# New places for every step of a fused cross-attention and mixture-of-experts kernel, and a second buffer for the softmax quotients

## The reference

```
x = x + xattn(layernorm(x), ctx, ctx)      # 16 heads of 16 features, one shared k and v
   c = concat([ctx, ctx]); k, v = split(c @ w_kv); softmax(q k / 4) v @ w_concat
x = x + ffn(layernorm(x))
   a = layer_norm(x) * nw + nb
   expert = argmax(softmax(a @ wg))        # 8 experts, 256 places each, in order of the tokens
   moe = gate * (gelu(a[expert's tokens] @ inter_w[e] + inter_b[e]) @ output_w[e] + output_b[e])
   res = gelu(a @ res_inter_w + b1) @ res_output_w + b2          # residual MLP, all tokens
   out = res * coef0 + moe * coef1 + x     # coef = softmax(a @ res_coef)
```

## Time and profile before

| | |
|---|---|
| median of 3 runs | 447.14 us (445.47 to 448.82) |
| profiled execution | 447.72 us, of which the trace's span is 446.0 us |
| busy share of the span | PE 86%, PEld 66%, DVE 32%, ACT 38%, POOL 34% |
| TensorE clock granted, mean | 0.924 of full |
| DMA | 49.78 MB, mean 112 GB/s |

### The profile page before, as it was taken

The page is one execution under the profiler, slowest core; times in us unless marked ns, Lnnn a source line. Parts: engine busy times, 40 slices in busy tenths (PEclk is TensorE's granted clock), DMA queues, the critical chain, the costliest instruction groups (busy, mean ns, idle before and its releaser), DMA issues.

```text
span 446.0 us, 5656 instructions
## 1 busy us (share of the span) xinstructions
PE 381.6 (86%) x1978; PEld 292.7 (66%) x1978; DVE 142.2 (32%) x461; ACT 167.6 (38%) x325; POOL 153.2 (34%) x219
## 2 busy tenths in 40 slices
PE   4767777778998788988988988889999899999992
PEld 2435245555676476576576566678888788888881
DVE  3263424532354354363364263241101010101020
ACT  3213334345255435534536525552243223332310
POOL 4322313218156238247238035265002121212122
PEclk9757666986999999998999999999999999999998
DMA  7678650230022462381411410085122775581212
GB/s 203 189 193 233 228 134 2 76 79 24 23 72 77 125 234 71 94 272 51 114 35 61 104 37 12 21 294 165 47 68 64 196 235 166 128 251 12 25 18 29
DMA packets 51331, 49.78 MB, mean 112 GB/s; under 512 B 4764, under 2 KB 48488, under 8 KB 51304
## 3 DMA queue, kind: packets, MB, share of 16 engines
q1 hardware_dynamic: 48232, 45.21, 33.2%
q0 software_dynamic: 3072, 4.21, 5.2%
HBM read 33.65 MB, written 15.63 MB: 111 GB/s over the span
## 4 chain that ended last, share of the span: by engine, by line
PE 65%; DMA 10%; ACT 8%; DVE 7%; issue 5%; POOL 2%; SPq 2%; DVEq 0%; POOLq 0%; ACTq 0%
PE mbank L776 20%; PE ubank L612 18%; PE mbank L612 11%; DMA drow<-dispatched 8%; PE mbank L607 4%; PE pbank L697 4%; ACT p L847 3%; PE sbank L665 3%; PE sbank L687 3%; DVE smax L977 3%; PE pbank L706 2%; DVE core L1021 2%; ACT h L890 1%; DMA wq_raw<-in_L_xattn_w_q 1%; ACT oT L791 1%
## 5 line engine op out<-in xcount | busy, mean ns | idle before, releaser
L890 ACT ACTIVATE h<-ubank,vecT 128x256 f32<-128x256 f32 x128 | 53.7, 471 | 131.7 <-PE ubank L612 131.7
L776 PE MATMUL mbank<-w2r,h 128*128 128x256 f32 x256 | 64.1, 390 | 0.5 <-ACT h L890 0.5
L612 PE MATMUL ubank<-ao,w1r 128*128 128x256 f32 x256 | 62.7, 393 | 0.0
L776 PE MATMUL mbank<-w2e,h 128*128 128x256 f32 x256 | 60.8, 379 | 0.0
L580 POOL DMA_INDIRECT out_rows<-yrow,rowid x16 | 24.8, 1548 | 103.7 <-DVE yrow L1097 73.5
L612 PE MATMUL ubank<-ao,w1e 128*128 128x256 f32 x256 | 60.0, 379 | 0.0
L776 PEld LDWEIGHTS mbank<-w2r,h 128*128 128x128 f32 x256 | 48.4, 194 | 12.8 <-issue 5.3
L612 PEld LDWEIGHTS ubank<-ao,w1r 128*128 128x128 f32 x256 | 49.4, 197 | 6.6
L612 PEld LDWEIGHTS ubank<-ao,w1e 128*128 128x128 f32 x256 | 48.5, 190 | 6.6
L776 PEld LDWEIGHTS mbank<-w2e,h 128*128 128x128 f32 x256 | 48.2, 190 | 6.3
L977 DVE TENSOR_REDUCE smax<-sbank 128x4 f32<-128x512 f32 x64 | 41.9, 685 | 26.5 <-PE sbank L665 26.2
(11 more groups left out here) (123 smaller groups left out, 438.1 us busy)
## 6 DMA issues: line engine op xcount, KB each, us to landing
w1e<-in_L_ffn_inter_w SPq DMA_DIRECT2D x8, 1024.0 KB, 4.9
w2e<-in_L_ffn_output_w SPq DMA_DIRECT2D x8, 1024.0 KB, 8.4
qstack<-dram_q SPq DMA_DIRECT2D x16, 384.0 KB, 4.6
dram_q<-qpart SPq DMA_DIRECT2D x8, 384.0 KB, 2.5
dispatched<-zrow SPq DMA_DIRECT2D x4, 516.0 KB, 5.4
drow<-dispatched SPq DMA_DIRECT2D x8, 258.0 KB, 8.3
xs<-in_x SPq DMA_DIRECT2D x8, 256.0 KB, 4.6
ctxs<-in_ctx SPq DMA_DIRECT2D x8, 256.0 KB, 4.7
```

The costliest lines, as they stand in the source:

```text
L612: last = nc.tensor.matmul(dst, w[kc], v[kc], start=(kc == 0), stop=(kc == len(w) - 1))
L776: last = nc.tensor.matmul(b[:, 0:D], h[:, n % 2, f, t * P:(t + 1) * P], w2[:, f, :], start=(f == 0), stop=(f == FC - 1))
L890: nc.scalar.activation(h[:, n % 2, f, :], place["up", n, c][:, j, :], ACT.Gelu_apprx_tanh, bias=vecT[:, col:col + 1]).then_inc(sem("gelu_d ...
```

## The change

All tables of places, the shifts per engine and the places of the weight loads get new numbers; no step is added or taken away, and no instruction of TensorE, ACT or POOL changes. `o_rec` becomes a double buffer, and VectorE waits, before the reciprocal of half n, for the product of half n - 2. The diff, with the tables for tiles 0 and 1 and four of the five shift tables left out:

```diff
-    PERIOD = 32.0
-    OWN = [0.0, 15.16, 39.23, 67.63]
+    PERIOD = 32.21
+    OWN = [0.0, 14.33, 41.69, 73.4]
...
     AT = {
-        "load": [-76.7], "ln1": [-54.8], "xn": [-52.25], "ctxT": [-41.9], "xT": [-40.87], "kv": [-40.43],
-        "q": [-38.6], "qrest": [-38.13], "qmid": [-37.44], "qlast": [-34.08], "vt": [-34.97],
-        "A": [-16.17, -16.03, -13.98, -13.7, -12.14, -10.48, -10.21, -9.82], "M": [-14.15, -7.57],
-        "B": [-0.63, 1.24, 3.97, 4.13, 7.09, 8.2, 10.73, 12.79],
-        "PV": [5.63, 14.29], "part": [7.43, 16.09], "o": [7.83, 16.49], "oT": [17.79],
-        "proj": [18.79], "ln2": [21.72], "core": [23.76], "gate": [30.12], "loc": [39.86], "gw": [16.86],
-        "bias": [23.76], "up": [17.62, 19.37, 22.16, 25.97],
-        "down": [-0.9, 1.07, 1.42, 4.34, 7.37, 8.31, 11.9, 14.56], "kspill": [-35.58],
-        "qspill": [-39.35, -37.87, -37.05], "gather": [-31.09, -28.45],
+        "load": [-79.74], "ln1": [-63.27], "xn": [-50.13], "ctxT": [-48.04], "xT": [-45.19], "kv": [-42.33],
+        "q": [-40.39], "qrest": [-40.09], "qmid": [-39.1], "qlast": [-39.74], "vt": [-37.99],
+        "A": [-18.06, -16.74, -15.42, -14.72, -13.92, -13.31, -11.95, -10.83], "M": [-34.32, -10.5],
+        "B": [-0.44, 0.05, 2.98, 3.65, 6.41, 7.29, 8.23, 11.35], "PV": [7.09, 14.78], "part": [12.73, 16.11],
+        "o": [11.31, 15.15], "oT": [17.9], "proj": [19.56], "ln2": [18.73], "core": [23.68], "gate": [28.22],
+        "loc": [36.57], "gw": [12.03], "bias": [-27.15], "up": [17.29, 20.49, 22.55, 25.66],
+        "down": [-0.66, 0.71, 0.83, 4.43, 5.56, 9.79, 11.69, 15.58], "kspill": [-42.25],
+        "qspill": [-41.17, -41.04, -31.06], "gather": [-34.12, -28.45],
     }
...
     LAG_SP = {
-        "load": [0.0], "kspill": [0.18], "qspill": [0.0], "gather": [0.0], "M": [0.0], "wload": [0.0],
-        "ein": [0.0], "down": [0.25], "zero": [0.0], "late": [-0.64],
+        "load": [-3.06], "kspill": [-1.11], "qspill": [0.29], "gather": [3.78], "M": [-0.96], "wload": [1.51],
+        "ein": [1.22], "down": [0.86], "zero": [0.25], "late": [0.96], "small": [7.41], "end": [-1.82],
     }
     LOADS = {
-        "late": [-70.79], "vec": [-39.4], "zero": [-46.04, -45.13, -6.03, -0.66],
-        "weights": [0.5, 14.17, 15.87, 27.03, 27.11],
+        "late": [-103.98], "vec": [-54.72], "zero": [-67.38, -31.9, -9.19, 21.09],
+        "weights": [24.83, 27.63, 29.55, 73.96, 85.37],
     }
...
-        "period": 17.22, "up": [-2.35, 2.53, 4.67, 9.02],
-        "down": [17.16, 18.79, 20.45, 21.34, 23.58, 25.85, 26.32, 28.49], "ein": [9.47], "first": [-3.51],
+        "period": 23.05, "up": [-7.01, -6.86, -4.49, 0.18],
+        "down": [7.0, 10.93, 19.81, 20.46, 25.14, 25.66, 26.43, 28.03], "ein": [21.21], "first": [-4.28],
...
-        o_rec = sb("o_rec", [P, HB, HB], f32, att)
+        o_rec = sb("o_rec", [P, 2, HB, HB], f32, att)
...
-                V.reciprocal(o_rec[:, :, :], b[:, :, :, DH]).then_inc(sem("o_root"), 1)
+                if n >= 2:
+                    dve.wait_ge(sem("o_ready"), n - 1)
+                V.reciprocal(o_rec[:, n % 2, :, :], b[:, :, :, DH]).then_inc(sem("o_root"), 1)
```

More of the change, by code:

```diff
@@ L61, in xattn_moe_ffn_kernel @@
     AT0 = {
-        "load": [-77.76], "ln1": [-59.31], "xn": [-52.55], "ctxT": [-55.73], "xT": [-54.86], "kv": [-39.85],
-        "q": [-39.27], "qrest": [-41.07], "qmid": [-36.79], "qlast": [-29.31], "vt": [-38.49],
[3 rows of a table removed]
[L67 to L70, removed]
+        "load": [-44.59], "ln1": [-98.81], "xn": [-67.28], "ctxT": [-88.29], "xT": [-57.74], "kv": [-36.77],
@@ L71, in xattn_moe_ffn_kernel @@
+        "q": [-36.83], "qrest": [-47.74], "qmid": [-31.9], "qlast": [-34.13], "vt": [-30.08],
[4 rows of a table added]
+        "down": [-3.0, -2.05, -0.61, 3.58, 7.49, 9.08, 9.74, 11.33], "kspill": [-55.01],
+        "qspill": [-61.59, -52.53, -50.27], "gather": [-32.5, -30.85],
     }
     AT1 = {
-        "load": [-99.55], "ln1": [-62.36], "xn": [-50.95], "ctxT": [-42.13], "xT": [-38.36], "kv": [-40.31],
-        "q": [-34.66], "qrest": [-39.25], "qmid": [-28.22], "qlast": [-34.73], "vt": [-30.34],
[3 rows of a table removed]
-        "proj": [18.79], "ln2": [21.77], "core": [23.95], "gate": [26.61], "loc": [39.06], "gw": [14.41],
@@ L79, in xattn_moe_ffn_kernel @@
-        "bias": [19.65], "up": [15.33, 16.98, 19.62, 23.21],
-        "down": [-0.9, 1.35, 1.75, 5.08, 8.54, 10.31, 13.7, 20.67], "kspill": [-40.66],
-        "qspill": [-42.52, -35.18, -34.88], "gather": [-34.05, -30.97],
+        "load": [-78.91], "ln1": [-63.14], "xn": [-50.13], "ctxT": [-47.99], "xT": [-43.13], "kv": [-41.61],
+        "q": [-40.4], "qrest": [-40.02], "qmid": [-39.39], "qlast": [-34.71], "vt": [-39.35],
[4 rows of a table added]
+        "down": [1.83, 3.79, 6.38, 9.23, 11.03, 29.12, 33.61, 33.64], "kspill": [-34.83],
@@ L82, in xattn_moe_ffn_kernel @@
+        "qspill": [-42.68, -41.49, -32.51], "gather": [-34.12, -28.45],
     }
     AT = {
-        "load": [-76.7], "ln1": [-54.8], "xn": [-52.25], "ctxT": [-41.9], "xT": [-40.87], "kv": [-40.43],
-        "q": [-38.6], "qrest": [-38.13], "qmid": [-37.44], "qlast": [-34.08], "vt": [-34.97],
[3 rows of a table removed]
-        "proj": [18.79], "ln2": [21.72], "core": [23.76], "gate": [30.12], "loc": [39.86], "gw": [16.86],
-        "bias": [23.76], "up": [17.62, 19.37, 22.16, 25.97],
-        "down": [-0.9, 1.07, 1.42, 4.34, 7.37, 8.31, 11.9, 14.56], "kspill": [-35.58],
@@ L95, in xattn_moe_ffn_kernel @@
     LAG_PE = {
-        "core": [0.0], "gate": [0.0], "loc": [0.06], "A": [0.0], "B": [0.0], "PV": [0.0], "part": [0.0], "up": [0.0],
-        "down": [0.0], "oT": [0.0], "proj": [0.0], "M": [0.61], "q": [0.0], "kv": [0.0], "vt": [0.0], "xT": [0.0],
-        "ctxT": [0.0], "ein": [0.0],
+        "core": [0.63], "gate": [0.79], "loc": [1.54], "A": [0.52], "B": [-0.68], "PV": [-0.25], "part": [0.0],
+        "up": [0.13], "down": [-0.05], "oT": [0.27], "proj": [0.0], "M": [1.58], "q": [-0.07], "kv": [-0.52],
@@ L99, in xattn_moe_ffn_kernel @@
+        "vt": [-0.48], "xT": [-0.38], "ctxT": [0.0], "ein": [-0.25], "vec": [-5.08],
     }
     LAG_ACT = {
-        "core": [0.0], "gw": [0.0], "B": [0.0], "PV": [0.0], "up": [0.0], "oT": [0.0], "M": [0.0], "q": [0.0], "kv": [0.0],
-        "xT": [-0.1], "ctxT": [0.0], "qmid": [0.18], "ein": [-1.35],
+        "core": [0.81], "gw": [-3.49], "B": [-0.66], "PV": [-0.37], "up": [0.0], "oT": [-1.15], "M": [0.04],
+        "q": [-0.55], "kv": [-1.34], "xT": [0.56], "ctxT": [0.24], "qmid": [0.13], "ein": [0.86], "small": [-0.77],
@@ L103, in xattn_moe_ffn_kernel @@
     }
     LAG_DVE = {
-        "core": [0.0], "gate": [0.53], "loc": [0.0], "A": [0.0], "gw": [0.0], "o": [0.0],
-        "proj": [0.0], "M": [-0.17], "vt": [0.0], "ln1": [0.0], "ln2": [0.0], "down": [0.0], "ein": [0.06],
-        "qrest": [-0.39],
+        "core": [-1.9], "gate": [0.72], "loc": [1.28], "A": [0.13], "gw": [-0.58], "o": [1.53], "proj": [-0.46],
+        "M": [1.49], "vt": [-0.11], "ln1": [0.35], "ln2": [0.82], "down": [0.0], "ein": [1.02], "qrest": [0.36],
+        "qlast": [0.0], "vec": [-4.54], "small": [0.0], "xn": [0.67],
@@ L108, in xattn_moe_ffn_kernel @@
     }
     LAG_POOL = {
-        "core": [0.09], "gw": [0.0], "kv": [1.06], "ln1": [2.16], "ln2": [0.0], "xn": [2.09], "bias": [0.0],
-        "down": [-1.44], "qlast": [0.0],
+        "core": [4.45], "gw": [-1.7], "kv": [-3.37], "ln1": [1.23], "ln2": [-0.78], "xn": [-1.87], "bias": [3.18],
+        "down": [-0.75], "qlast": [-2.5], "end": [0.03], "small": [-0.08],
     }
     LAG_SP = {
-        "load": [0.0], "kspill": [0.18], "qspill": [0.0], "gather": [0.0], "M": [0.0], "wload": [0.0],
-        "ein": [0.0], "down": [0.25], "zero": [0.0], "late": [-0.64],
+        "load": [-3.06], "kspill": [-1.11], "qspill": [0.29], "gather": [3.78], "M": [-0.96], "wload": [1.51],
@@ L993, in o @@
                 b = place["part", u, t][:, :, :].rearrange("p i (j x) -> p j i x", j=HB)
-                V.reciprocal(o_rec[:, :, :], b[:, :, :, DH]).then_inc(sem("o_root"), 1)
+                if n >= 2:
+                    dve.wait_ge(sem("o_ready"), n - 1)
+                V.reciprocal(o_rec[:, n % 2, :, :], b[:, :, :, DH]).then_inc(sem("o_root"), 1)
                 dve.wait_ge(sem("o_root"), n + 1)
                 V.tensor_tensor(o_rows[:, t, :].rearrange("p (j i d) -> p j i d", j=HB, i=HB), b[:, :, :, 0:DH],
-                                o_rec[:, :, :].unsqueeze(3).broadcast_to([P, HB, HB, DH]), ALU.mult)\
+                                o_rec[:, n % 2, :, :].unsqueeze(3).broadcast_to([P, HB, HB, DH]), ALU.mult)\
                     .then_inc(sem("o_ready"), 1)
```

## The result

The changed kernel takes **414.31 us**, median of 4 runs (413.43 to 416.42), against 447.98 (445.47 to 449.90) for the kernel before in the same comparison: ratio 0.926, 95% interval 0.920 to 0.932. The forecast of 424.4 had the right side and its range holds the time, but 10 us of the gain were not in it.

The account below looks back on a forecast made before the run. The prediction took TensorE as the bound throughout, with only idle time and lost clock to win. Steady part -18.0, weights +5.9, tiles 0 and 1 -12, start -4 and experts +4.8 took 447.7 to 424.4 us, range 411 to 439.

Parts of the forecast that it names:

- The steady part: Rounds from up 2.0 to up 6.0: stops at PV, proj, A, core and q go, -18.0 us before the weights' cost.
- The tight place at xT: xT 6 needs POOL's xn, now behind the scatter, ready some 0.3 us ahead; half a microsecond may be lost.
- my sign of being wrong: In the new trace, the forecast is wrong if a steady round, expected at 28.5 us, is still 33 us.
- Weights ahead of the gather: On SP's queue, A 5.0 and A 6.0 wait about 2.0 to 2.2 us each, +4.2, plus half clock, +1.7.
- rival 2: Transfers are not held behind the weights: no stop at A 5.0, A 6.0 or ein 1; 411 us, chance 0.10.
- Tiles 0 and 1: Gate 0 to up 2.0: three large stops at oT 1, core 1 and PV 2.0 go, -12 us (0 to -17).
- Start to gate 0: First 82 us: small losses on loads, cover for about half of ten stops; -4 us (bounds +3 and -10).
- rival 4: Weights cost their full landing at B 2.0, A 5.0, A 6.0 and ein 1; slower, 457 us, chance 0.07.
- Experts: From up 8.0: ein 1 waits behind weights, +5.4, half clock +1.7; ein 3 to 6 gain 2.3; net +4.8 us.
- o_rec: The wait on o_rec costs nothing, as the product it waits for is complete before part starts.
- 1 fell: Rival: the early part, first 155.9 us, keeps its length and only 3 us are won there; 437 us, chance 0.20.
- 3 fell: Rival: a POOL chain bound replaces the stops, the steady part gains nothing, tiles 0 and 1 half; 448 us, chance 0.08.

Follow-up runs that it names:

- e1_w01: The changed kernel with the weights of experts 0 and 1 issued behind a tile's gathers again, as before the change: 406.42 us, ratio 0.913 to the kernel before.
- e14_wr: e13_best with the residual MLP's weights issued right behind M 0.1, ahead of M 1, on SP alone: 390.75 us, ratio 0.881 to the kernel before.
- e7_fill_before: The kernel before, orders untouched, with 223 small unread matmuls ahead of 24 early steps where TensorE waits: 438.78 us, ratio 0.978.
- e6_fill_after: The changed kernel with 139 small unread matmuls ahead of twelve steps of the first 52 us: 415.54 us, ratio 0.928 to the kernel before.
- e13_best: The changed kernel with all five weight loads moved on SyncE: residual MLP's ahead of load 4, experts' 0 to 3 put back: 397.91 us, ratio 0.889 to the kernel before.
- e15_wr_fill: e14_wr with 139 small unread filler matmuls on TensorE in the first part: 391.29 us, ratio 0.882 to the kernel before.
- e3_orec: The changed kernel with a single buffer for the quotients and without the added wait, orders as changed: 414.71 us, ratio 0.926 to the kernel before.

## Why the prediction was right, and where it was not

- **The steady part, right.** Without the weights ahead of the gathers (e1_w01) up 2.0 to up 6.0 went from 129.5 to 110.2 us, -19.3 against the forecast -18.0. Core, proj and q stand without brackets, and the round not touched by weights, from 194.0 to 222.5, is 28.4 us (forecast 28.5). The tight place at xT cost nothing, which is about the 1.0 I took off. The two rounds with weights are 32.6 and 32.7 us, where I had 31 to 32. That is close to my sign of being wrong ("still 33 us"), and e1_w01, where they are 28.7, shows that only the weights keep them there.
- **Weights ahead of the gather, right in mechanism, a little small.** Stops of 2.37 and 2.88 us where I had 2.0 to 2.2; two stretches of half clock where I had one. The Trainium skill (DMA: Bandwidth & Descriptors, Queues, rings and completion order) has one row's descriptors consumed in ring order; the same 128 KB landing in 7.9 us behind 2 MB and in 3.6 without agree with it. This refutes rival 2, whose 411 lies nearer to the time than my sum, by another way.
- **Tiles 0 and 1: the stops right, the number by luck.** The three stops are gone. What I did not see is a new stop of 2.62 us in that stretch, at up 0.0, on w2r. The -11.6 for -12 is the two together: in e14_wr, where w2r is in time, the stretch is 57.8 us, -16.1, near my bound of -17. As up 0.0 waits for w2r whenever gate 0 comes, the cut at gate 0 splits one quantity. From the start to up 2.0 it is -27.2 for my -16.
- **Start to gate 0: the step that failed.** I put -4 on it, with -10 as the lower bound, and it was -15.6. That working priced stops alone: idle time did fall, by 5.3 us, about what it said. The clock had no term, and busy time fell by 10.3. e7_fill_before shows what clock is worth in the old order, 8.5 us up to gate 0 in these profiles without a single step moved. Fillers in the new order are worth 4.8 against the changed kernel's profile (0.3 to 5.6 against the five without fillers), and with fillers in both the new order is still 11.9 us ahead (61.56 for 73.47). As e7_fill_before keeps one stretch of half clock, 25.0 to 35.3 us, and e6_fill_after has none there, up to 5 of these 11.9 can be clock too. So of 15.6 us between 3.7 and about 9 are clock, the rest shorter waits. These bounds are no sharper than the profiles: gate 0 is at 78.05 to 81.97 in the three of the old order and at 61.81 to 67.19 in the five of the new one without fillers. What each compute engine's order gives was not separated. My one sentence with the Trainium skill (TensorE: Matmul & The Clock Gate, Part 1, sustained activity releases the clock) pointed the right way, to 420; the fillers, with which the mean clock up to gate 0 is 0.93 in the old order and not 0.71, agree with it. That the lower clock is the default is not in rows 1, which I called a witness: their first digit is a 9. The durations do agree with it. The first row below is the kernel before from 0 to 10 us, and its clock is given as 1.00; but the first four transposes of `ctxs` take 1.09 us, and the same four later take 0.66. So the granted clock that is given for the first microseconds is too high here, and the changed kernel's trace has the same (1.08 and 0.60 us):

```profile
0.00:10.00 10.00, 4.02 (x12) 2.17 (x12) 3.86 (x17) 3.43 (x5) 4.24 (x19) 1.00 0.67 188
```

```profile
4.50 1.09 PE L607 MATMUL mbank<-ident,ctxs 128*128 128x128 f32 x4 [4.50 <-DMA ctxs<-in_ctx]
...
15.41 0.66 PE L607 MATMUL mbank<-ident,ctxs 128*128 128x128 f32 x4
```

- **The residual MLP's weights: overlooked.** I followed `wload` -1 to B 2.0 (rival 4) and not to up 0.0. Moved from 40.8 us, between other loads, to 59.3, its second matrix landed at 70.3. e13_best to e14_wr, a move of this pair alone, is 7.2 us between the medians and 7.9 in the traces at up 0.1 (76.90 to 68.99). The two stand in different comparisons, and the intervals of their ratios overlap; but the slowest of the 8 runs of e14_wr and e15_wr_fill, 394.20, is below the fastest of e13_best, 396.07. So the early part of the change could have been worth 7 to 9 us more (up 0.1 is at 77.86 after the change), and this loss hid in the total how far my -4 was off.
- **Experts, right in mechanism.** ein 1 waits 6.12 us for 5.4, and drow lands 10.8 us after its issue; with the half clock from 295.2 to 300.6 it is 8.1 for 7.1. The gain at ein 3 to 6 (forecast -2.3) shows in e14_wr: 114.6 us for 116.6, -2.0.
- **o_rec, right:** 0 (e3_orec).
- **Rivals.** 1 fell with the table's first row. 3 fell: no stop of TensorE after the change is put down to POOL. 4 fell in size: A 5.0 and A 6.0 cost 8.3 us, ein 1 cost 8.1, and up 0.0, in place of B 2.0, up to 8.9: 25, not 46. That 414.3 lies inside the range is partly luck. Start to up 2.0 won 11 us more than I had even with the stop at up 0.0. By my estimate from the 7.9 us above, the time would have been about 406 without that stop, below the range.
